# Three changes in one: two steps laid out in the program before the loop, transposes from a norm written in reverse, and fuller filler matmuls behind the first adder

## The chip, the cores and the metric

The kernel runs on one core of a Trainium2 chip. The metric is device time in microseconds (us) of one execution, as the median of three runs. Every value is float32 on a grid of 128 partitions: 4 images times 32 channels; a token is one of the 784 pixels.

## The reference

Four residual blocks follow each other on `x` of shape (4, 32, 28, 28):

```
x = x + conv_block(ln(x))       # 1x1 conv, adder 1 (-sum |x - w|), bn, relu, 3x3 conv, adder 2 (3x3), bn, relu
t = tokens(x); t = t + chain(ln(t))
x = x + quantised_convs(ln(x))  # two 3x3 convs with fake quantisation
t = tokens(x); t = t + stu(ln(t))   # 16 causal filters over time, then mixed by matrices; plus 3 lags

def step(h, p):                 # chain: a scan over 33 blocks
    op = argmax(h[0, 0, :19])
    y = attention(h, p, op);  h = where(p.am[op], y, h)
    z = ffn(h, p, op);        h = where(p.fm[op], z, h)
```

In the chain a block changes `h` only where its masks are set for the operation that the state itself picks. With these inputs two blocks change it: the first with its feed-forward part alone, the second with attention and feed-forward. The third decision says that nothing is left.

## The kernel before, in words

Each engine runs its own instruction stream, and semaphores order them. SP issues most DMAs, GpSimd sets up constants, and all matmuls are issued by the helper `mm` (L905), so that nearly every TensorE row of the profile carries that line. A float32 matmul stands in the trace as two weight loads and two matmuls.

**Adder 1 and what follows.** `group(g)` (L959) sums eight rings of `max(x, w)` or `|x - w|` into banks 6 and 7. A product of one column signals `adder_done`, and `SHORT` = 7 more of them follow (L980). ScalarE turns the banks into `H1P` (L369), and 9 taps of a convolution read `H1P` (L984 to L990, 144 matmul rows). Its result is copied by ScalarE (L374) and VectorE (L716), and 72 groups of adder 2 follow. `keep_warm(n)` issues n full filler products of 128x128 by 128x196, whose result nobody reads.

**The steps.** VectorE's `decide` (L763) writes a code into `KINT`: 0 for nothing left, bit 0 for attention, bit 1 for feed-forward. SP, ScalarE, VectorE and TensorE each load it into a register and walk `active_steps` (L74 to L89): three nested hardware loops of 3, 4 and 3 passes, with an `If(code > 0)` at each level, and the body of a step inside the innermost. The body stands once in each engine's program. After the last step the loops still run out: the innermost goes round once more, the middle one three times, the outer one twice, each pass branching over what is inside. In the body, `If((c & 1) > 0)` (L1030 on TensorE, L793 on VectorE, L412 on ScalarE) branches over the attention part when its bit is not set; `If((c & 2) > 0)` (L1133 on TensorE) does so for feed-forward. SP's `fetch` (L248) reads the code and issues the DMAs of the step's weights: `W4R` (L257), `W1R` (L261), `W2S` (L263). At the end of a step each engine waits for `decided`, loads the code again (L1155, L1156 on TensorE) and goes round. Behind the loops ScalarE loads the table for the square root (L465), and TensorE begins `norm(2)` with the product with `CEN` (L933), which needs `x2_ready` from VectorE's `residual` (L778).

**The last block.** `norm(3)` on VectorE (L532) writes its result in two halves into `UPZ`, in order of time. ScalarE writes it reversed into `URV` (L478), and TensorE transposes eight pieces of `URV` into banks 4 and 5 (L1185 to L1189), four for each parity. ScalarE and VectorE copy the two banks into `UT` (L482, L888). Then TensorE runs `filtered(u)` for 64 units and `mixed(grp)` for 16 groups into banks 6 and 7. SP builds `ULAG` from `UPZ` by 12 DMAs once `ln_out` has reached 8 (L279); they are read at group 12. After `mixed(15)` VectorE adds banks 6 and 7 to the residual (L899), and SP stores the result.

Of the kernel before, what the change touches and what calls it, by code (L numbers as in the profile page):

```python
# [4 lines left out]

# [1 line left out]

# [11 lines left out]
ACT = mybir.ActivationFunctionType  # L19
# [3 lines left out]
P = 128  # L23
NIMG, C, SIDE = 4, 32, 28
T = SIDE * SIDE
QU = T // 4
HT = T // 2
# [1 line left out]
PS_ = SIDE + 2  # L29
PADF = 904  # L30
NB, NOPS, HID = 33, 19, 128
STEPS = (3, 4, 3)

WARM = dict(inputs=6, means=4, squares=2, deviations=4, choice=8, weights=8, exponentials=2, sums=2, copies=11, evictions=3, relus=4, values=3)
SHORT = 7
OPW = 1024
QT, NQ = 112, 7
NK = 16
# [32 lines left out]
DVE_UPTO = [g - a for g, a in enumerate(ACT_UPTO)]  # L71


@contextmanager  # L74
def active_steps(e, code):


    assert STEPS[0] * STEPS[1] * STEPS[2] >= NB
    with e.Fori(0, STEPS[0]):
        with e.If(e.snap(code, min_val=0, max_val=4 * NB + 7) > 0):  # L80
            with e.Fori(0, STEPS[1]):
                with e.If(e.snap(code, min_val=0, max_val=4 * NB + 7) > 0):
                    with e.Fori(0, STEPS[2]):
                        c = e.snap(code, min_val=0, max_val=4 * NB + 7)
                        with e.If(c > 0):
                            yield c
                        e.nop()
                e.nop()
        e.nop()  # L89


def build(nc, x, par, con, ws1, wa1c, wa1r, ws2, wa2c, wa2r, amt, fmt, fwa, fwb, aw,
          cw1, cw2, phe, pho, mpp, mpm, mu, out):
    with ExitStack() as ctx:
# [6 lines left out]
        PS = ctx.enter_context(nc.psum_tensor("PS", [P, 8, 512], F32))  # L101
# [8 lines left out]
        X1 = sb("X1", [P, T]); HSUM = sb("H", [P, PS_ * SIDE]); H = HSUM[:, 0:T]  # L110
# [29 lines left out]
        UT = WS2[:, 0:8, :]  # L140
# [27 lines left out]
        def half(ap, h):  # L168
            return ap[:, h * HT:(h + 1) * HT]
# [9 lines left out]
        def bank(b, w=HT, rows_=slice(0, P)):  # L179
            return PS[rows_, b, 0:w]  # L180
# [17 lines left out]
        def by_image(src, n, c0=0, w=None):  # L198
# [12 lines left out]
            "wexp w_fill w_soft u_mixed w_chain sg_ready d_chain d_ready lags_in ut_done ut_ready urv_ready u_done uev_act uev_dve mix_done y_ready stored"  # L211
# [6 lines left out]
        def _(sp):  # L218
# [25 lines left out]
            code = sp.alloc_register("sp_code"); which = sp.alloc_register("sp_which")  # L244
# [21 lines left out]
            sp.wait_ge(s["decided"], 1)  # L266
            fetch()
            sp.reg_mov(chosen, 1)
            with active_steps(sp, code):
                n = sp.snap(chosen, min_val=1, max_val=NB)  # L270
                sp.wait_ge(s["decided"], n + 1)
                sp.sem_inc(s["sp_woke"], 1)
                sp.reg_add(chosen, chosen, 1)
                fetch()

            sp.wait_ge(s["ln_out"], 8)
            for b in range(NIMG):
                for lag in range(3):
                    sp.dma_start(ULAG[32 * lag:32 * lag + 32, b, :], UPZ[32 * b:32 * b + 32, 2 - lag:2 - lag + T]).then_inc(s["lags_in"], 16)  # L279
# [49 lines left out]
        def _(a):  # L329
# [49 lines left out]
            for n in range(9 * CQ):  # L379
# [10 lines left out]
                if n in (63, 66):  # L390
                    i = (n - 63) // 3
# [19 lines left out]
            with active_steps(a, code) as c:  # L411
                with a.If((c & 1) > 0):  # L412
                    k = a.snap(na, min_val=0, max_val=NB)

# [47 lines left out]
                a.load(code, KINT[0:1, 0:1], bass_reorder=False)  # L462
                a.reg_mov(code, a.snap(code) & (OPW - 1))

            a.activation(WSM[:, 44:45], con_("eps6", 1), ACT.Sqrt)  # L465
            norm(2, "eps6")

# [3 lines left out]
                    a.activation(half(SQ, h), bank(4 + h), ACT.Relu, bias=QS[:, 10 + i:11 + i],  # L471
                                 scale=QS[:, 8 + i:9 + i]).then_inc(s["cv_relu"], 1)
            norm(3, "eps5")
            a.wait_ge(s["zeroed"], 5)
            for h in range(2):
                a.wait_ge(s["ln_out"], 6 + h + 1)
                lo = h * HT
                a.activation(URV[:, 1024 - lo - HT:1024 - lo], UPZ[:, 2 + lo + HT - 1:2 + lo - 1:-1],  # L478
                             ACT.Copy).then_inc(s["urv_ready"], 1)

            a.wait_ge(s["ut_done"], 1)
            a.activation(UT[:, 0:4, :], PS[:, 4, 0:512].rearrange("p (i m) -> p i m", i=4), ACT.Copy).then_inc(s["ut_ready"], 1)  # L482
            for u in range(0, 64, 2):
                a.wait_ge(s["u_done"], u + 1)
                if u >= 8:
# [5 lines left out]
        def _(v):  # L491
# [23 lines left out]
            def norm(k, src, dst, between=None, after=None):  # L515

                for h in range(2):
                    if k == 0:
                        v.wait_ge(s["ln_mean"], h + 1)
                        v.tensor_tensor(half(XC, h), half(src, h), bank(h), ALU.subtract).then_inc(s["ln_cent"], 1)  # L520
                    else:
                        v.wait_ge(s["ln_sq"], 2 * k + h + 1)
                        v.tensor_copy(half(XC, h), bank(h)).then_inc(s["ln_cent"], 1)
                if between:
                    between()
                v.wait_ge(s["ln_sd"], k + 1)
# [263 lines left out]
            with active_steps(v, code) as c:  # L790
                past()
                look_ahead()
                with v.If((c & 1) > 0):  # L793
# [62 lines left out]
                v.load(code, KINT[0:1, 0:1], bass_reorder=False)  # L856
                v.reg_mov(code, v.snap(code) & (OPW - 1))

            norm(2, X, lambda h: half(XN, h))

            def hold(src, recip, low, high, tmp):
# [21 lines left out]
                v.tensor_tensor(X1[:, :], X[:, :], RS[:, :], ALU.add).then_inc(s["x3_sum"], 1)  # L883

            v.wait_ge(s["zeroed"], 5)
            norm(3, X1, lambda h: UPZ[:, 2 + h * HT:2 + (h + 1) * HT], None, summed)
            v.wait_ge(s["ut_done"], 2)
            v.tensor_copy(UT[:, 4:8, :], PS[:, 5, 0:512].rearrange("p (i m) -> p i m", i=4)).then_inc(s["ut_ready"], 1)  # L888
            for u in range(1, 64, 2):
                v.wait_ge(s["u_done"], u + 1)  # L890
                if u >= 8:
                    v.wait_ge(s["mix_done"], u // 4 - 1)
                v.tensor_copy(UEV[:, u % 8, :], bank(u % 6)).then_inc(s["uev_dve"], 1)  # L893
            v.wait_ge(s["mix_done"], 16)
            v.wait_ge(s["x3_sum"], 1)
            x3 = X1[:, :].rearrange("p (t a) -> p t a", a=2)
            y = Y1[:, :].rearrange("p (t a) -> p t a", a=2)
            for a2 in range(2):
                v.tensor_tensor(y[:, :, a2], x3[:, :, a2], bank(6 + a2), ALU.add).then_inc(s["y_ready"], 1)  # L899


        @block.tensor
        def _(t):
            def mm(out_, lhsT, rhs, start=True, stop=True):
                return t.matmul(out_, lhsT, rhs, start=start, stop=stop, skip_group_check=True)  # L905

            def keep_warm(n, src=CON, b=3):

                for _ in range(n):
                    mm(bank(b, QU), src[:, 0:P], src[:, 0:QU])  # L910
# [66 lines left out]
            for g in range(CQ):  # L977
                group(g)
            mm(PS[0:1, 5, 500:501], CON[:, 0:1], CON[:, 0:1]).then_inc(s["adder_done"], 1)
            for _ in range(SHORT):  # L980
                mm(PS[0:1, 5, 500:501], CON[:, 0:1], CON[:, 0:1])
            t.wait_ge(s["ws_rep"], 10)
            t.wait_ge(s["h1_ready"], 2)
            for tap in range(9):  # L984
# [43 lines left out]
            with active_steps(t, code) as c:  # L1028
                keep_warm(WARM["weights"])
                with t.If((c & 1) > 0):  # L1030
                    k, n = t.snap(na, min_val=0, max_val=NB), t.snap(chosen, min_val=1, max_val=NB)
# [10 lines left out]
                    for u in range(2 * NQ):  # L1042
                        j, h = u // 2, u % 2
# [111 lines left out]
                t.load(code, KINT[0:1, 0:1], bass_reorder=False)  # L1155
                t.reg_mov(code, t.snap(code) & (OPW - 1))  # L1156

            n = t.snap(chosen, min_val=1, max_val=NB + 1)
            t.wait_ge(s["x2_ready"], n)
            norm(2, X)  # L1160
# [183 lines left out]
```

## Time and profile before

| | us |
|---|---|
| median of 3 runs (384.72 to 385.14) | 384.8 |
| the profiled execution, its own time | 383.83 |
| its span, first to last instruction | 382.0 |
| TensorE matmuls busy | 346.2 (91%) |
| VectorE busy | 231.9 (61%) |
| ScalarE busy | 166.1 (43%) |

The span is taken apart by the profile; 1.8 us of the execution's own time lie outside it. The chain of waits is the path, followed back from the last instruction, of what released what. Busy time of TensorE holds fillers too, so it says little of what bounds the kernel. The granted clock is the share of full speed that TensorE was given: 1.0 is 2.4 GHz and 0.5 is 1.2 GHz.

### The profile page before, as it was taken

To read this page: it belongs to the slowest core of one execution; us is meant where nothing else is said; L and a number is where in the kernel's file an instruction comes from. 1 tells how busy PE (TensorE), PEld (TensorE's weight loads), DVE (VectorE), ACT (ScalarE), POOL (GpSimd) and SP (SyncE) were. 2 spreads that over 40 slices of the span, in tenths; PEclk is the share of its full clock that TensorE was granted. 3 is DMA by queue.
4 is the path that set the end of the run, shared out by engine and by line. 5 is a ranking of instruction groups with operands and counts; after the bars stand their busy time and mean duration, and the time that the engine had idled before them with its cause. 6 is when DMAs were issued, how large, how long until landed. Compare 5 with 4: busy or idle time off the path is not lost.

```text
span 382.0 us, 11465 instructions
## 1 busy us (share of the span) xinstructions
PE 346.2 (91%) x5075; PEld 201.3 (53%) x5075; DVE 231.9 (61%) x287; ACT 166.1 (43%) x161; POOL 20.2 (5%) x40
## 2 busy tenths in 40 slices
PE   8898999999999998695579998578799999999995
PEld 7535547743333346471153343454566667677773
DVE  2787999999999986559975785256411112121112
ACT  2851897888898931430018775213211111111110
POOL 4490000000000011000000000000000000000000
PEclk9998999999999999999999999899999999999998
DMA  5618000000000009000000000000320000000001
GB/s 164 213 22 307 33 2 2 2 2 3 2 2 2 2 8 330 16 16 2 0 2 2 0 2 2 0 2 0 72 58 3 3 3 3 3 3 3 3 3 44
DMA packets 10184, 12.79 MB, mean 33 GB/s; under 512 B 4102, under 2 KB 8984, under 8 KB 10136
## 3 DMA queue, kind: packets, MB, share of 16 engines
q1 hardware_dynamic: 9160, 8.85, 7.5%
q0 software_dynamic: 832, 3.00, 2.3%
q8 instruction: 42, 0.69, 0.7%
q10 hardware_dynamic: 144, 0.20, 0.2%
q14 instruction: 6, 0.05, 0.0%
HBM read 10.44 MB, written 0.40 MB: 28 GB/s over the span
## 4 chain that ended last, share of the span: by engine, by line
PE 76%; DVE 9%; issue 6%; DMA 2%; ACT 2%; SPq 1%; DVEq 0%; ACTq 0%
PE PS L905 76%; DVE TOPS L800 4%; DVE RSC L527 1%; DMA W1R<-in_fwa 1%; DMA W4R<-in_aw 1%; DVE pool_ L849 1%; DVE TMP L716 1%; DVE pool_ L744 0%; DVE pool_ L568 0%; ACT pool_ L438 0%; ACT SDC L338 0%; ACT H1P L369 0%; DVE X L759 0%; DVE TMP L757 0%; SPq L250 0%
## 5 line engine op out<-in xcount | busy, mean ns | idle before, releaser
L905 PE MATMUL PS<-pool_,CON 128*32 128x392 f32 (+2 forms) x1320 | 110.2, 493 | 0.6 <-DVE pool_ L744 0.4
L396 ACT ACTIVATE pool_<-TMP,WA 128x3136 f32<-128x3136 f32 x27 | 78.1, 2924 | 12.2 <-PE PS L905 11.4
L744 DVE TENSOR_SCALAR pool_<-TMP,WA 128x3136 f32<-128x3136 f32 x45 | 81.3, 1849 | 0.1
L905 PEld LDWEIGHTS PS<-pool_,CON 128*32 128x32 f32 (+1 forms) x1320 | 49.5, 110 | 59.2 <-issue 46.4
L893 DVE COPY pool_<-PS 128x392 f32<-128x392 f32 x32 | 18.1, 567 | 83.2 <-PE PS L905 83.2
L487 ACT ACTIVATE pool_<-PS 128x392 f32<-128x392 f32 x32 | 15.9, 498 | 85.0 <-PE PS L905 85.0
L905 PE MATMUL PS<-HE,WS 128*32 128x136 f32 (+3 forms) x1024 | 46.3, 333 | 0.8 <-DVE WS L888 0.8
L905 PE MATMUL PS<-pool_,WS 128*32 128x136 f32 (+3 forms) x1024 | 46.3, 333 | 0.0
L905 PEld LDWEIGHTS PS<-HE,WS 128*32 128x32 f32 x1024 | 31.9, 110 | 15.8 <-issue 10.8
L905 PEld LDWEIGHTS PS<-pool_,WS 128*32 128x32 f32 x1024 | 32.1, 110 | 14.8 <-issue 10.8
L905 PE MATMUL PS<-CON 128*128 128x196 f32 (+2 forms) x208 | 37.1, 323 | 2.1 <-DVE TOPS L800 0.8
L905 PEld LDWEIGHTS PS<-CON 128*128 128x128 f32 (+1 forms) x208 | 32.6, 184 | 10.2 <-issue 6.3
L438 ACT ACTIVATE pool_<-PS 112x896 f32<-112x896 f32 (+1 forms) x28 | 21.6, 822 | 6.3 <-PE PS L905 6.3
L800 DVE TENSOR_REDUCE TOPS<-PS 112x4 f32<-112x1568 f32 x14 | 23.9, 1783 | 0.3 <-PE PS L905 0.3
L905 PE MATMUL PS<-Y,QZ 32*112 32x392 f32 x112 | 12.9, 532 | 9.5 <-DVE TOPS L800 9.5
L821 DVE TENSOR_TENSOR pool_<-pool_ 112x1792 f32<-112x1792 f32 (+1 forms) x9 | 16.3, 1810 | 5.2 <-ACT pool_ L438 5.1
L905 PE MATMUL PS<-QZ,Y 32*112 32x448 f32 (+1 forms) x112 | 15.7, 531 | 0.3 <-ACT pool_ L438 0.3
L905 PE MATMUL PS<-pool_,ASEG 128*32 128x49 f32 (+2 forms) x512 | 14.4, 248 | 0.1
L905 PEld LDWEIGHTS PS<-Y,QZ 32*112 32x112 f32 x112 | 4.0, 169 | 18.4 <-DVE TOPS L800 17.2
L905 PE MATMUL PS<-pool_,VT 112*32 112x448 f32 (+1 forms) x112 | 12.0, 502 | 0.0
L420 ACT ACTIVATE VT<-PS 112x896 f32<-112x896 f32 x1 | 0.9, 918 | 25.1 <-PE PS L905 25.1
L905 PEld LDWEIGHTS PS<-QZ,Y 32*112 32x112 f32 x112 | 6.1, 169 | 9.2 <-issue 6.5
(215 smaller groups left out, 287.2 us busy)
## 6 DMA issues: line engine op xcount, KB each, us to landing
pool_<-in_pho SPq DMA_DIRECT2D x1, 3144.0 KB, 11.7
HE<-in_phe SPq DMA_DIRECT2D x1, 3136.0 KB, 10.4
QZ<-CW SPq DMA_DIRECT2D x12, 98.0 KB, 2.2
CW<-in_cw POOLq DMA_DIRECT2D x2, 576.0 KB, 4.7
CON<-in_con POOLq DMA_DIRECT2D x1, 732.5 KB, 5.6
out_y<-Y SPq DMA_DIRECT2D x1, 392.0 KB, 3.0
CQ<-in_ws SPq DMA_DIRECT2D x16, 9.0 KB
MPP<-in_mpp POOLq DMA_DIRECT2D x1, 256.0 KB, 2.9
```

The source lines that it names most:

```text
L396: a.activation(RING[:, g % RG, :, :].rearrange("p b (r c) -> p b r c", r=SIDE), window(n // CQ), ACT.Abs, bias=WA2[:, n:n + 1], scale=-1.0 ...
L420: a.activation(VT[0:QT, :, :], PS[0:QT, 4:8, 0:C * NQ], ACT.Copy).then_inc(s["v_done"], 1)
L438: a.activation(PT[0:QT, st % PR, 2 * pair:2 * pair + 2, 0:QC[ch]], PS[0:QT, 2 * (u % 3):2 * (u % 3) + 2, 0:QC[ch]], ACT.Exp, scale=SCALE). ...
L487: a.activation(UEV[:, u % 8, :], bank(u % 6), ACT.Copy).then_inc(s["uev_act"], 1)
L527: v.reciprocal(RSC[:, :], SDC[:, :]).then_inc(s["ln_rs"], 1)
L716: v.tensor_copy(inner(0, 1, 4)[64 * c:64 * c + 64], PS[64:128, 0:4, 0:HT].rearrange("p b (r c) -> p b r c", r=HROWS)).then_inc(s["y2_ready ...
L744: v.tensor_scalar(RING[:, g % RG, :, :].rearrange("p b (r c) -> p b r c", r=SIDE), window(n // CQ), WA2[:, n:n + 1], None, ALU.max).then_i ...
L800: v.tensor_reduce(TOPS[0:QT, u, :], PS[0:QT, 4 - 4 * (u % 2):8 - 4 * (u % 2), 0:HT], AX.X, ALU.max).then_inc(s["top_step"], 1)
L821: v.tensor_tensor(ACC[0:QT, :, 0:w], PT[0:QT, (st - 1) % PR, :, 0:w] if i == 1 else ACC[0:QT, :, 0:w], PT[0:QT, st % PR, :, 0:w], ALU.add) ...
L849: v.tensor_scalar(HIDT[:, u, :], bank(u), B1S, 0.0, ALU.add, ALU.max).then_inc(s["hid_dve"], 1)
L893: v.tensor_copy(UEV[:, u % 8, :], bank(u % 6)).then_inc(s["uev_dve"], 1)
L905: return t.matmul(out_, lhsT, rhs, start=start, stop=stop, skip_group_check=True)
```

## The change

Three edits are made together.

1. `active_steps` takes the body as a function and emits it three times: twice in a row, each behind an `If(code > 0)`, and a third time inside two nested loops (4 and 8 passes), all of it inside the second `If`'s successor. A code of 0 after the second step branches over the loops and the third copy.
2. `norm(3)` writes its result reversed, straight into `URV`. TensorE transposes the first piece of each parity after the first half (`ln_out` 7), the other six after the second. It starts the filters when ScalarE's half of `UT` is there, and waits for VectorE's half at unit 4. ScalarE writes `UPZ` from `URV` afterwards, in one instruction, and SP's 12 DMAs wait for that. At the end, the addition of bank 6 waits for `mixed(13)` only.
3. Behind adder 1, four full filler products replace seven of one column.

```diff
-STEPS = (3, 4, 3)
+STEPS = (4, 8)
-def active_steps(e, code):
-    with e.Fori(0, STEPS[0]):
-        with e.If(e.snap(code, min_val=0, max_val=4 * NB + 7) > 0):
-            with e.Fori(0, STEPS[1]):
-                with e.If(e.snap(code, min_val=0, max_val=4 * NB + 7) > 0):
-                    with e.Fori(0, STEPS[2]):
-                        c = e.snap(code, min_val=0, max_val=4 * NB + 7)
-                        with e.If(c > 0):
-                            yield c
-                        e.nop()
-                e.nop()
-        e.nop()
+def active_steps(e, code, step):
+    def taken():
+        return e.snap(code, min_val=0, max_val=4 * NB + 7)
+    with e.If(taken() > 0):
+        step(taken())
+        with e.If(taken() > 0):
+            step(taken())
+            with e.If(taken() > 0):
+                with e.Fori(0, STEPS[0]):
+                    with e.If(taken() > 0):
+                        with e.Fori(0, STEPS[1]):
+                            c = taken()
+                            with e.If(c > 0):
+                                step(c)
+                            e.nop()
+                    e.nop()
...
 # SP, before the 12 DMAs
-            sp.wait_ge(s["ln_out"], 8)
+            sp.wait_ge(s["u_plain"], 1)
...
 # ScalarE
             norm(3, "eps5")
-            a.wait_ge(s["zeroed"], 5)
-            for h in range(2):
-                a.wait_ge(s["ln_out"], 6 + h + 1)
-                lo = h * HT
-                a.activation(URV[:, 1024 - lo - HT:1024 - lo], UPZ[:, 2 + lo + HT - 1:2 + lo - 1:-1],
-                             ACT.Copy).then_inc(s["urv_ready"], 1)
             a.wait_ge(s["ut_done"], 1)
-            a.activation(UT[:, 0:4, :], ...).then_inc(s["ut_ready"], 1)
+            a.activation(UT[:, 0:4, :], ...).then_inc(s["ut_act"], 1)
+            a.wait_ge(s["zeroed"], 5)
+            a.wait_ge(s["ln_out"], 8)
+            a.activation(UPZ[:, 2:2 + T], URV[:, 1023:1023 - T:-1], ACT.Copy).then_inc(s["u_plain"], 1)
...
 # VectorE
-            norm(3, X1, lambda h: UPZ[:, 2 + h * HT:2 + (h + 1) * HT], None, summed)
+            norm(3, X1, lambda h: URV[:, 1023 - h * HT:1023 - (h + 1) * HT:-1], None, summed)
...
-            v.wait_ge(s["mix_done"], 16)
             for a2 in range(2):
+                v.wait_ge(s["mix_done"], 14 + 2 * a2)
                 v.tensor_tensor(y[:, :, a2], x3[:, :, a2], bank(6 + a2), ALU.add).then_inc(s["y_ready"], 1)
...
 # TensorE
-            for _ in range(SHORT):
-                mm(PS[0:1, 5, 500:501], CON[:, 0:1], CON[:, 0:1])
+            keep_warm(WARM["shifts"], b=5)      # WARM["shifts"] = 4
...
-            t.wait_ge(s["ln_out"], 8)
-            t.wait_ge(s["urv_ready"], 2)
+            t.wait_ge(s["ln_out"], 7)
             for c in range(2):
-                for i in range(4):
-                    a0 = 1024 - 255 - c - 256 * i
-                    last = mm(PS[:, 4 + c, P * i:P * i + P], URV[:, a0:a0 + 255:2], con_("ident"))
+                turned(c, 0)
+            t.wait_ge(s["ln_out"], 8)
+            for c in range(2):
+                for i in range(1, 4):
+                    last = turned(c, i)
                 last.then_inc(s["ut_done"], 1)
-            t.wait_ge(s["ut_ready"], 2)
             t.wait_ge(s["strip_in"], 32)
+            t.wait_ge(s["ut_act"], 1)
...
+                if u == 4:
+                    t.wait_ge(s["ut_dve"], 1)
```

`turned(c, i)` is the transpose that stood in the loop before.

## Rows read from the trace of the kernel before

**Rows 1.** The chain that ended last; columns: start us, us, what.
```profile
44.44 97.42 PE PS L905 x1159
...
157.13 1.52 issue
...
165.61 3.04 DMA W4R<-in_aw
...
241.66 4.12 issue
...
275.14 101.37 PE PS L905 x2230
```
**Rows 2.** Timeline of TensorE's matmuls behind adder 1: start us, us.
```profile
28.69 0.54 PE L905 MATMUL PS<-CON 128*1 128x1 f32 x16
30.83 7.88 PE L905 MATMUL PS<-H1P,WS 32*64 32x392 f32 x144 [1.60 <-ACT H1P L369]
```
**Rows 3.** Busy time by stretch; after POOL stand PEclk, DMA share, GB/s.
```profile
31.20:34.50 3.30, 3.30 (x49) 1.95 (x41) 3.02 (x13) 0.00 (x0) 0.00 (x0) 0.50 1.04 383
34.60:38.60 4.00, 4.00 (x104) 2.27 (x88) 1.85 (x7) 0.00 (x0) 0.00 (x0) 1.00 1.06 391
```
**Rows 4.** Timeline of TensorE, four full filler products at full clock.
```profile
146.89 1.59 PE L905 MATMUL PS<-CON 128*128 128x196 f32 x8
```
**Rows 5.** Timeline of VectorE, the first copy after the convolution.
```profile
38.88 1.79 DVE L716 COPY TMP<-PS 64x1568 f32<-64x1568 f32 x1 [2.29 <-PE PS L905]
```
**Rows 6.** TensorE's sequencer in front of step 1, by line: min/median/max ns, start us.
```profile
L80 PEldq COMPARE_BRANCH  x1: 94/94/94, 153.3 to 153.3; - x1
...
L85 PEldq COMPARE_BRANCH  x1: 65/65/65, 153.9 to 153.9; - x1
...
L1030 PEldq COMPARE_BRANCH  x1: 3832/3832/3832, 154.2 to 154.2; - x1
```
**Rows 7.** Busy time and instructions in step 2: its attention, then all of it.
```profile
168.60:234.50 65.90, 54.73 (x567) 22.71 (x567) 50.20 (x40) 27.15 (x38) 0.00 (x0) 1.00 0.01 2
165.40:241.00 75.60, 63.24 (x632) 28.99 (x632) 56.71 (x53) 31.38 (x45) 0.00 (x0) 1.00 0.01 3
```
**Rows 8.** The loops' end on TensorE's sequencer (first and last line) and DMA, 236 to 256.
```profile
L83 PEldq COMPARE_BRANCH  x2: 76/150/223, 240.7 to 241.4; - x2
...
L79 PEldq COMPARE_BRANCH  x3: 76/207/208, 244.1 to 245.6; - x3
...
DMA packets 0, 0.00 MB, mean 0 GB/s; under 512 B 0, under 2 KB 0, under 8 KB 0
```
**Rows 9.** Timeline of ScalarE behind the loops.
```profile
244.22 1.28 ACT L465 ACT_TABLE_LOAD   x1 [4.78 <-issue]
```
**Rows 10.** Two products with CEN in norm 2, and the same two in norm 3.
```profile
245.79 2.60 PE L905 MATMUL PS<-X,CEN 128*128 128x392 f32 x4 [4.12 <-issue]
...
258.69 1.48 PE L905 MATMUL PS<-X,CEN 128*128 128x392 f32 x4
```
**Rows 11.** Busy time and clock behind the loops, columns as in rows 3.
```profile
246.20:249.60 3.40, 3.40 (x8) 1.98 (x6) 1.14 (x2) 1.00 (x2) 0.00 (x0) 0.50 0.00 0
```
**Rows 12.** Timelines of TensorE, VectorE and ScalarE between norm 3 and the filters.
```profile
272.23 2.12 PE L905 MATMUL PS<-CON,CW 128*128 128x128 f32 x16 [1.31 <-ACT CW L478]
...
270.30 1.23 DVE L532 TENSOR_TENSOR CW<-TMP,PS 128x392 f32<-128x392 f32 x2 [0.20 <-PE PS L905]
274.39 0.69 DVE L888 COPY WS<-PS 128x512 f32<-128x512 f32 x1 [2.87 <-PE PS L905]
...
270.95 1.14 ACT L478 ACTIVATE CW<-CW 128x392 f32<-128x392 f32 x2 [3.09 <-DVE CW L532]
273.45 0.60 ACT L482 ACTIVATE WS<-PS 128x512 f32<-128x512 f32 x1 [1.36 <-PE PS L905]
```
**Rows 13.** Timeline of VectorE at the end.
```profile
375.89 0.57 DVE L893 COPY pool_<-PS 128x392 f32<-128x392 f32 x1 [2.23 <-PE PS L905]
377.55 1.04 DVE L899 TENSOR_TENSOR Y<-X,PS 128x392 f32<-128x392 f32 x2 [1.09 <-PE PS L905]
```

More of the change, by code:

```diff
@@ L8 @@
-from contextlib import ExitStack, contextmanager
+from contextlib import ExitStack
 import concourse.bass as bass
@@ L31 @@
 NB, NOPS, HID = 33, 19, 128
-STEPS = (3, 4, 3)
-WARM = dict(inputs=6, means=4, squares=2, deviations=4, choice=8, weights=8, exponentials=2, sums=2, copies=11, evictions=3, relus=4, values=3)
-SHORT = 7
+STEPS = (4, 8)
+WARM = dict(inputs=6, means=4, squares=2, deviations=4, choice=8, weights=8, exponentials=2, sums=2, copies=11, evictions=3, shifts=4, relus=4, values=3)
 OPW = 1024
@@ L71 @@
 DVE_UPTO = [g - a for g, a in enumerate(ACT_UPTO)]
-@contextmanager
-def active_steps(e, code):
-    assert STEPS[0] * STEPS[1] * STEPS[2] >= NB
-    with e.Fori(0, STEPS[0]):
-        with e.If(e.snap(code, min_val=0, max_val=4 * NB + 7) > 0):
-            with e.Fori(0, STEPS[1]):
-                with e.If(e.snap(code, min_val=0, max_val=4 * NB + 7) > 0):
-                    with e.Fori(0, STEPS[2]):
-                        c = e.snap(code, min_val=0, max_val=4 * NB + 7)
-                        with e.If(c > 0):
-                            yield c
-                        e.nop()
-                e.nop()
-        e.nop()
+def active_steps(e, code, step):
+    def taken():
+        return e.snap(code, min_val=0, max_val=4 * NB + 7)
+    assert 2 + STEPS[0] * STEPS[1] >= NB
+    with e.If(taken() > 0):
[11 more added lines that the diff above has]
+                    e.nop()
 def build(nc, x, par, con, ws1, wa1c, wa1r, ws2, wa2c, wa2r, amt, fmt, fwa, fwb, aw,
@@ L210, in build @@
             "wmx_part wmx_rows wmx_row wmx_bc q_sc q_chain cq_chain cq_done x2_ready q_xin cc_done cv_relu cv_q x3_ready x3_sum "
-            "wexp w_fill w_soft u_mixed w_chain sg_ready d_chain d_ready lags_in ut_done ut_ready urv_ready u_done uev_act uev_dve mix_done y_ready stored"
+            "wexp w_fill w_soft u_mixed w_chain sg_ready d_chain d_ready lags_in ut_done ut_act ut_dve u_plain u_done uev_act uev_dve mix_done y_ready stored"
         ).split()}
@@ L268, in _, with step @@
             sp.reg_mov(chosen, 1)
-            with active_steps(sp, code):
+            def step(c):
                 n = sp.snap(chosen, min_val=1, max_val=NB)
@@ L274, in _ @@
                 fetch()
-            sp.wait_ge(s["ln_out"], 8)
+            active_steps(sp, code, step)
+            sp.wait_ge(s["u_plain"], 1)
             for b in range(NIMG):
@@ L410, in _, with step @@
             a.reg_mov(chosen, 1)
-            with active_steps(a, code) as c:
+            def step(c):
                 with a.If((c & 1) > 0):
@@ L463, in _ @@
                 a.reg_mov(code, a.snap(code) & (OPW - 1))
+            active_steps(a, code, step)
             a.activation(WSM[:, 44:45], con_("eps6", 1), ACT.Sqrt)
@@ L473, in _ @@
             norm(3, "eps5")
+            a.wait_ge(s["ut_done"], 1)
+            a.activation(UT[:, 0:4, :], PS[:, 4, 0:512].rearrange("p (i m) -> p i m", i=4), ACT.Copy).then_inc(s["ut_act"], 1)
             a.wait_ge(s["zeroed"], 5)
-            for h in range(2):
-                a.wait_ge(s["ln_out"], 6 + h + 1)
-                lo = h * HT
-                a.activation(URV[:, 1024 - lo - HT:1024 - lo], UPZ[:, 2 + lo + HT - 1:2 + lo - 1:-1],
-                             ACT.Copy).then_inc(s["urv_ready"], 1)
-            a.wait_ge(s["ut_done"], 1)
-            a.activation(UT[:, 0:4, :], PS[:, 4, 0:512].rearrange("p (i m) -> p i m", i=4), ACT.Copy).then_inc(s["ut_ready"], 1)
+            a.wait_ge(s["ln_out"], 8)
+            a.activation(UPZ[:, 2:2 + T], URV[:, 1023:1023 - T:-1], ACT.Copy).then_inc(s["u_plain"], 1)
             for u in range(0, 64, 2):
@@ L789, in _, with step @@
             v.reg_mov(na, 0); v.reg_mov(nf, 0)
-            with active_steps(v, code) as c:
+            def step(c):
                 past()
@@ L857, in _ @@
                 v.reg_mov(code, v.snap(code) & (OPW - 1))
+            active_steps(v, code, step)
             norm(2, X, lambda h: half(XN, h))
@@ L885, in _ @@
             v.wait_ge(s["zeroed"], 5)
-            norm(3, X1, lambda h: UPZ[:, 2 + h * HT:2 + (h + 1) * HT], None, summed)
+            norm(3, X1, lambda h: URV[:, 1023 - h * HT:1023 - (h + 1) * HT:-1], None, summed)
             v.wait_ge(s["ut_done"], 2)
-            v.tensor_copy(UT[:, 4:8, :], PS[:, 5, 0:512].rearrange("p (i m) -> p i m", i=4)).then_inc(s["ut_ready"], 1)
+            v.tensor_copy(UT[:, 4:8, :], PS[:, 5, 0:512].rearrange("p (i m) -> p i m", i=4)).then_inc(s["ut_dve"], 1)
             for u in range(1, 64, 2):
@@ L1027, in _, with step @@
             t.reg_mov(chosen, 1)
-            with active_steps(t, code) as c:
+            def step(c):
                 keep_warm(WARM["weights"])
@@ L1156, in _ @@
                 t.reg_mov(code, t.snap(code) & (OPW - 1))
+            active_steps(t, code, step)
             n = t.snap(chosen, min_val=1, max_val=NB + 1)
@@ L1182, in direct, with turned @@
                 return last
-            t.wait_ge(s["urv_ready"], 2)
+            def turned(c, i):
+                a0 = 1024 - 255 - c - 256 * i
+                return mm(PS[:, 4 + c, P * i:P * i + P], URV[:, a0:a0 + 255:2], con_("ident"))
+            t.wait_ge(s["ln_out"], 7)
             for c in range(2):
-                for i in range(4):
-                    a0 = 1024 - 255 - c - 256 * i
-                    last = mm(PS[:, 4 + c, P * i:P * i + P], URV[:, a0:a0 + 255:2], con_("ident"))
+                turned(c, 0)
[3 more added lines that the diff above has]
+                    last = turned(c, i)
                 last.then_inc(s["ut_done"], 1)
-            t.wait_ge(s["ut_ready"], 2)
             t.wait_ge(s["strip_in"], 32)
+            t.wait_ge(s["ut_act"], 1)
             def filtered(u):
```

## The prediction, made before the changed kernel ran

> **What bounds the kernel now.** I read the page for the busy shares, then the chain of waits, then the timelines, sequencer rows and granted clock at each of the three places that the change touches. On the chain the reader should see two kinds of piece. Adder 2 is one TensorE piece of 97.42 us and the filters one of 101.37 us [rows 1]: nothing in the change touches their inside, so a microsecond gained ahead of either arrives whole at the end. Between them lie short serial stretches, and two of the longest waits there are called "issue": 1.52 us before the first feed-forward and 4.12 us behind the last step [rows 1]. The sequencer's rows say what these are. In front of step 1, TensorE's branch over the attention part took 3.832 us [rows 6], against 65 and 94 ns for branches not taken. Behind step 2 the loops run out in a dozen branches of 76 to 223 ns, from 240.7 to 245.7, and no DMA packet moves meanwhile [rows 8]: their targets were on the engine already. So a branch costs either about 0.2 us or nearly 4, and the question of this change is which kind the new exit is.
>
> **Fillers behind adder 1.** Removed are seven products of one column, which with the signal take 0.54 us and end at 29.23; TensorE then waits 1.60 us for `H1P` and starts at 30.83 [rows 2]. From 31.2 to 34.5 it is granted half its clock, later all of it [rows 3]. Four full fillers take 1.59 us [rows 4]; from about 28.76 (one eighth of the 0.54 is the signal's) they end at 30.35, still 0.48 before the convolution can start, so they cost nothing. Past that cover each further filler would cost 0.4. They leave a gap of 0.5 us instead of 1.6, and I expect the clock to hold. At half clock 41 weight loads passed in 3.30 us, at full clock 88 in 4.00 or a little less, since they stop before the stretch ends [rows 3]: 0.045 us each, so the 41 would take 1.86 at most and 1.65 at exactly double speed. The gain is 1.44 to 1.65. Bounds: nothing, if the clock falls anyway, and 1.65. The copies behind find their engine free: VectorE idled 2.29 us before its one [rows 5]. I take **1.6**, since a convolution that only TensorE carries should follow its clock.
>
> **Entering step 1.** The loop set-up between the branches at L80 (153.3) and L85 (153.9) goes [rows 6]: 0.6 us. The branch over attention stays, over the same distance, and its 3.83 us begin 0.6 earlier. TensorE is ready at 158.05 instead of 158.65. The weights landed at 157.13 [rows 1], so they don't take the place of the stall until 1.5 us are gone. Gain **0.6**; bounds 0 (the fetch ends no earlier) and 1.5 (the landing). Between the steps nothing is gained: step 2 starts when `W4R` lands, 3.04 us after its issue at 165.61 [rows 1], SP issues it inside the body, and TensorE's fillers cover the loop's turn.
>
> **Leaving step 2.** The dozen branches become one move and one branch at about 240.65. Its target lies behind a third copy of the body. Step 2 executed 632 matmuls and as many weight loads, its attention part alone 567 of each [rows 7]. The branch that skipped those 567 pairs was not resident and took 3.83 us; this one skips 632 pairs, code that never ran. I therefore price it at the same 3.83: it ends at 244.48, and norm 2 starts 0.15 later, at 244.63, instead of 245.79 [rows 10]. Gain **1.16**. Bounds: with a resident target 0.2 us, so that TensorE starts at 241.75, after its last filler (the wait of 4.12 begins at 241.66 [rows 1]), gain 4.0; with a second fetch behind the first, up to another 3.83, loss 2.7. ScalarE loads its table at 244.22 [rows 9] and is ready at 245.7. In the new kernel a short jump there lets it load from 240.9; were its jump as long as TensorE's, it would still load at 244.2, and its first square needs TensorE's product, not before 245.4. VectorE and SP have more time than that. So TensorE sets it.
>
> The Trainium skill, page "Runtime: NRT & Kernel Launch", section "Instruction fetch mechanics", says that prefetch is sequential in blocks, and that a taken branch outside the current two pages stalls for a fetch. For the new exit that gives the same result as my 3.83. It also would make most backward and forward branches of the old exit stalls; this trace measured 76 to 223 ns for them, so here the measurement decides, and the old exit is priced at what it took.
>
> **The clock behind the exit.** The wait of 4.12 us was followed by half clock from 246.2 to 249.6 [rows 11]: the two products with `CEN` took 2.60 us, where norm 3's took 1.48 [rows 10]. The new wait is 3.0 us (241.66 to 244.63). A wait of 1.6 behind adder 1, after thin products, was enough for a fall. I take it to stay: **0**. If it doesn't, between 1.1 (the products alone) and 1.7 (half of 3.4) is gained; 1.4 is the middle.
>
> **Before the filters.** Now: VectorE's halves end at 270.87 and 271.53, ScalarE reverses the second until 272.10, eight transposes take 2.12 us from 272.23, VectorE's copy ends at 275.08 [rows 12], filters at 275.14 [rows 1]. New: the transposes of the first piece run from 271.0 to 271.5, beside VectorE's second half. From 271.63 the remaining six take 12 of 16 rows' time, 1.5. ScalarE's bank is complete after three (0.72 to the last start, 0.3 for it): its copy runs 272.65 to 273.25 (0.60 [rows 12]), and the filters start at 273.30. VectorE's copy of the other bank ends before 274.1 and is needed four units of 64 later, 6.3 of the 101.37 us. Gain **1.84**. The price of writing backwards on VectorE isn't in the trace; nearest is its last addition, which writes every second element at 0.52 us each for 392 [rows 13], and ScalarE's reversed read at 0.57. I take nothing; doubled writes would cost 1.2 at most. ScalarE's new whole write of `UPZ`, about 1.1 us by its two old ones [rows 12], ends at 274.4, before the first unit wants evicting, one 64th of 101.37 us behind 273.30, at 274.9. The 12 DMAs move about 2.8 us later; their data are read at group 12, some 75 us on, so they cost nothing, and it would take that much delay before they cost.
>
> **The end.** Bank 6's addition moves ahead of `mixed(15)`: VectorE is free at 376.46, the pair now starts at 377.55 and takes 1.04 [rows 13]. One of the two is hidden. Gain **0.5**; bounds 0 and 0.52.
>
> **The sum.** 1.6 + 0.6 + 1.16 + 0 + 1.84 + 0.5 = 5.7 us. The profiled execution of 383.83 (1.8 outside its span) becomes 378.1. The median of the runs lies 1.0 above that execution, so the median goes from 384.8 to 379.1.
>
> **Rivals.**
> - *The exit's target is resident.* For it: every branch of the old exit was. Against it: the skip over a shorter stretch in step 1 wasn't. TensorE starts 2.85 us sooner than forecast and idles too little for the clock to fall: 379.1 - 2.85 - 1.4 = 374.8. The skill's "Advanced Engine Details and Errata", section "ISA Cache", gives TensorE 128 KB; were code resident that far ahead, this would be the case.
> - *The clock holds behind the exit.* The wait is a quarter shorter. 379.1 - 1.4 = 377.7.
> - *The fillers don't hold the clock behind adder 1*, so the edit does not do what it could: 379.1 + 1.6 = 380.7. For it: a gap of 0.5 us stays; against it: that is a third of the old one, and the work ahead of it is no longer thin.
> - *A second fetch behind the exit.* The landing is near the end of a block, and the next one arrives late: up to 3.83 us more on the path, 381 to 383. Even whole it doesn't undo the sum.
> - *Slower: step 2's attention stalls on its own instructions.* It is now a second copy, reached in a straight line behind a first that was skipped. If it meets two stalls like that of [rows 6], 7.7 us are lost and the kernel ends at 384.8 - 5.7 + 7.7 = 386.8; one leaves it faster, the second decides. Against it: in the old kernel too its attention ran for the first time in step 2, and TensorE was busy there for 54.73 of 65.90 us [rows 7], which leaves little room for stalls.
>
> **Chances.** Forecast as it stands 0.48; clock holds behind the exit 0.17; fillers without effect 0.11; second fetch 0.10; resident target 0.07; slower or no gain by step 2's fetches 0.07. The range goes from 377.0 to 381.6: it holds the first three cases and the nearer part of the second fetch, about 0.8. Under 0.2% (0.77 us) this kernel's measurement cannot tell from no change. Faster 0.93, same 0.03, slower 0.04.
>
> **What would show it.** Clock 1.0 from 31 to 35, and the convolution at about 6.3 us instead of 7.88. A branch of about 3.8 us on TensorE at the new kernel's exit, an instruction packet within it, and norm 2 starting about 3 us after the last filler. Transposes in two pieces, and under 2.5 us from VectorE's first half to the filters, instead of 4.3. One addition behind the last matmul. Wrong it would be through a short exit branch, a second long branch or idle "issue" in norm 2, or "issue" inside step 2.

## The result and the profile after

The changed kernel took 379.56 us on the median of 4 executions (378.59 to 381.2), against 384.97 for the kernel before: a ratio of 0.9856 with a 95% interval of 0.9811 to 0.9900. The forecast was 379.1, in a range of 377.0 to 381.6, faster. With six further executions the changed kernel's median over ten is 379.03, and that of the kernel before over the 62 that ran beside the experiments is 384.70. The ratios, here and below, compare fast executions alone, those within 1.5% of the fastest of the same kernel. The single executions scatter far more than the three shown at first: those 62 lie between 380.33 and 387.82.

One number that comes with each execution orders most of this scatter: its mean granted clock. Of the 62, the twelve with 0.99 or more have a median of 381.24, the thirty with 0.98 or less one of 385.97. The profiled execution of the changed kernel took 381.2 at 0.964, the slowest of its four; the forecast for it had been 378.1. Its stages have to be compared one by one.

First the chain of the changed kernel, from the start of the convolution; columns as in [rows 1].

```profile
30.25 6.26 PE PS L915 x144
...
42.17 97.41 PE PS L915 x1159
...
154.87 1.03 issue
...
162.13 0.46 issue
...
163.38 3.15 DMA W4R<-in_aw
...
193.76 8.75 PE PS L915 x89
...
243.69 2.42 issue
...
273.62 101.39 PE PS L915 x2201
```

The two long pieces are as long as before [rows 1]. The convolution is 1.7 us shorter than in [rows 2]. Both "issue" pieces at the far branches are there, shorter, and one of 0.46 is new: SP pauses between reading the code and issuing the weights of step 2. Next TensorE's sequencer at the two far branches; columns as in [rows 6].

```profile
L1040 PEldq COMPARE_BRANCH  x1: 3917/3917/3917, 151.4 to 151.4; - x1
...
L84 PEldq COMPARE_BRANCH  x1: 3342/3342/3342, 242.6 to 242.6; - x1
```

The branches of the loops' end, of which [rows 8] show the first and last lines (15 by all of them, not the dozen of the prediction), have become one of 3.34 us. The DMA view from 242.6 to 246.0 holds this row: one instruction packet of 0.02 MB, and narrower windows place it between 243.5 and 243.7, inside the branch.

```profile
q8 instruction: 1, 0.02, 1.9%
```

ScalarE's, VectorE's and SP's own branches of the same line took 0.05, 0.056 and 0.045 us. The stall is TensorE's alone.

Then the clock, by stretch; columns as in [rows 3].

```profile
31.20:34.50 3.30, 3.30 (x88) 2.10 (x80) 3.02 (x15) 0.00 (x0) 0.00 (x0) 1.00 1.03 376
175.00:192.00 17.00, 15.27 (x80) 4.29 (x76) 16.57 (x11) 0.00 (x0) 0.00 (x0) 0.50 0.01 1
195.40:202.00 6.60, 6.60 (x40) 5.26 (x40) 1.81 (x8) 1.46 (x2) 0.00 (x0) 0.50 0.00 0
246.60:249.90 3.30, 3.30 (x8) 1.89 (x7) 1.13 (x2) 0.99 (x2) 0.00 (x0) 0.50 0.03 7
```

Behind adder 1 the clock holds now, 80 weight loads in a stretch that had 41 [rows 3]. In norm 2 it falls as before [rows 11]. New against the profile before is half clock for 17 us in the row maxima of attention and for nearly 7 behind them. Last, the end of norm 3 and of the kernel, in the timelines of TensorE, ScalarE and VectorE; these answer to [rows 12] and [rows 13].

```profile
271.21 2.35 PE L915 MATMUL PS<-CON,CW 128*128 128x128 f32 x16
273.62 5.75 PE L915 MATMUL PS<-HE,WS 128*32 128x392 f32 x125
...
272.88 0.60 ACT L486 ACTIVATE WS<-PS 128x512 f32<-128x512 f32 x1 [4.72 <-PE PS L915]
...
270.59 1.23 DVE L539 TENSOR_TENSOR CW<-TMP,PS 128x392 f32<-128x392 f32 x2 [0.19 <-PE PS L915]
273.59 0.69 DVE L898 COPY WS<-PS 128x512 f32<-128x512 f32 x1 [1.77 <-PE PS L915]
...
374.88 0.56 DVE L909 TENSOR_TENSOR Y<-X,PS 128x392 f32<-128x392 f32 x1
376.06 0.56 DVE L909 TENSOR_TENSOR Y<-X,PS 128x392 f32<-128x392 f32 x1 [0.61 <-PE PS L915]
```

Writing backwards costs VectorE nothing: 1.23 us for two halves, as in [rows 12]. The filters start 3.03 us after VectorE begins its first half; before it was 4.84.

Stage by stage, worked out from the starts and ends in both kernels' timelines (us):

| stage | before | after | difference | forecast |
|---|---|---|---|---|
| start to convolution | 30.83 | 30.25 | -0.58 | 0 |
| convolution | 7.88 | 6.19 | -1.69 | -1.6 |
| first decision to feed-forward | 6.84 | 6.39 | -0.45 | -0.6 |
| second decision to projections | 5.26 | 5.87 | +0.61 | 0 |
| projections to third decision | 70.67 | 74.82 | +4.15 | 0 |
| third decision to norm 2 | 6.11 | 4.41 | -1.70 | -1.16 |
| norm 2, to its last product | 7.93 | 7.90 | -0.03 | 0 |
| then to the filters | 21.42 | 19.61 | -1.81 | -1.84 |
| filters to the last addition's end | 103.45 | 102.99 | -0.46 | -0.5 |

With -0.01 over the stages not shown, this adds up to the 1.97 us by which the last addition ends sooner (378.59 to 376.62). The 0.58 at the start is no edit's gain: two profiles of the changed kernel have 30.25 and 30.47, and those of the kernels below lie between 30.21 and 31.25, with either kind of product behind adder 1. Nor is the rest of the profiled execution's gain (2.63 us in all): the store of the result landed 2.4 us after its issue instead of 3.0, and it took 2.4 or 2.5 in every kernel below, whatever its edits.

### The profile page after: what moved, and what is told of

The parts are those of the page before. It is cut to its first block, busy times and chain, and to the rows that moved or that the text cites. A ratio compares the mean times of both kernels' runs of the same rounds, so it can differ in the third digit from the quotient of the medians.

```text
span 379.4 us, 11303 instructions
## 1 busy us (share of the span) xinstructions
PE 354.3 (93%) x5069; PEld 211.7 (56%) x5069; DVE 231.5 (61%) x287; ACT 165.8 (44%) x160; POOL 19.6 (5%) x40
## 4 chain that ended last, share of the span: by engine, by line
PE 79%; DVE 8%; issue 4%; DMA 2%; ACT 1%; SPq 1%; DVEq 0%; ACTq 0%
PE PS L915 79%; DVE TOPS L808 3%; DVE RSC L534 1%; DMA W1R<-in_fwa 1%; DMA W4R<-in_aw 1%; DVE pool_ L857 1%; DVE TMP L723 1%; DVE pool_ L751 0%; DVE pool_ L575 0%; ACT pool_ L446 0%; ACT SDC L345 0%; ACT H1P L376 0%; DVE X L766 0%; DVE TMP L764 0%; SPq L254 0%
## 5 line engine op out<-in xcount | busy, mean ns | idle before, releaser
L915 PE MATMUL PS<-HE,WS 128*32 128x392 f32 (+3 forms) x1024 | 46.5, 333 | 0.1
L915 PE MATMUL PS<-CON 128*128 128x196 f32 (+1 forms) x202 | 40.2, 346 | 2.4 <-DVE TOPS L808 0.9
L915 PEld LDWEIGHTS PS<-pool_,WS 128*32 128x32 f32 x1024 | 35.8, 110 | 11.2 <-issue 3.5
L915 PEld LDWEIGHTS PS<-HE,WS 128*32 128x32 f32 x1024 | 35.6, 111 | 11.6 <-issue 4.1
L915 PEld LDWEIGHTS PS<-CON 128*128 128x128 f32 x202 | 35.2, 200 | 10.3 <-issue 5.4
L915 PE MATMUL PS<-Y,QZ 32*112 32x392 f32 x112 | 19.6, 786 | 3.6 <-DVE TOPS L808 3.4
L915 PE MATMUL PS<-QZ,Y 32*112 32x448 f32 (+1 forms) x112 | 16.6, 563 | 0.3 <-ACT pool_ L446 0.3
L915 PEld LDWEIGHTS PS<-Y,QZ 32*112 32x112 f32 x112 | 5.6, 241 | 17.5 <-DVE TOPS L808 16.4
```

## The experiments

The theory was: each edit acts by itself, the exit waits for a fetch of code that lies too far ahead, and the large remainder is TensorE's clock. The rivals: the exit waits for other things; the new layout itself brings the clock down in attention; the fillers' gain was chance.

**Each edit alone, on the kernel before.** The edits are the three parts of the diff in the section on the change.

> The kernel before with the filler edit alone. My account: the convolution behind adder 1 runs at full clock, in 6.2 us instead of 7.9, and the kernel gains 1.4 to 1.7 us (about 383.3). Rival: the low clock there was chance and the kernel before often runs without it; then the gain over many runs is under 0.5 us.

Measured: 383.99 us (12 executions, 382.42 to 387.6), ratio 1.0019 (0.9977 to 1.0061). Its profile has the convolution in 6.19 us; the timing can't tell a gain.

> The kernel before with the program's layout of the steps alone. My account, from the changed kernel's rows: about 0.45 us gained in front of step 1, about 0.6 lost between the steps, 1.2 to 1.7 gained at the exit, where TensorE's branch takes 3.3 to 3.9 us; together 1 to 1.7 us, about 383.5. Rival: the straight layout also causes the half clock in the row-max stage that the changed kernel's profile shows from 175 to 202 us; then this kernel is no faster on the median, and its mean clock is low in several runs.

Measured: 382.41 us (12 executions), ratio 0.9926 (0.9879 to 0.9972). In its profile 0.53 us are gained in front of step 1 and 0.49 lost between the steps; the exit branch is 3.62 us long, and the way from the decision to norm 2 takes 4.69 instead of 6.11. The row maxima ran at full clock, from 170 to 193 us:

```profile
170.00:193.00 23.00, 13.54 (x124) 4.12 (x116) 21.57 (x15) 0.81 (x3) 0.00 (x0) 1.00 0.00 1
```

So the layout doesn't bring the clock down there by itself. Behind the row maxima this profile has half clock too, from 195.5 to 201.5. The kernel with the filler edit alone, whose layout is the old one, shows the same fall there; the mean over 9 us is 0.62:

```profile
193.00:202.00 9.00, 9.00 (x92) 7.21 (x91) 3.13 (x8) 2.06 (x3) 0.00 (x0) 0.62 0.01 2
```

> The kernel before with the edits of the last block alone. My account: filters start 1.8 us sooner and the last addition ends 0.45 sooner, 2.3 us together, about 382.5, in every run alike since nothing of it hangs on the clock. Rival: the backward write or the later 12 DMAs cost something that the single profile hides; then under 1.8.

Measured: 381.88 us (12 executions), ratio 0.9966 (0.9923 to 1.0009), unclear as a time. In its profile both stages are as forecast: 19.62 us from norm 2 to the filters, 103.00 from there to the last addition. It also ran the convolution behind seven thin products, the case in which the clock was to fall, at full clock:

```profile
28.23 0.54 PE L902 MATMUL PS<-CON 128*1 128x1 f32 x16
30.36 6.19 PE L902 MATMUL PS<-H1P,WS 32*64 32x392 f32 x144 [1.58 <-ACT H1P L369]
```

By their medians the three kernels are 0.7, 2.3 and 2.8 us below the kernel before beside them (384.68). That adds up to 5.8, near the whole, but by the ratios only 3.4 us are found, and the scatter is too large to prove a sum. The terms are told apart by the stages of the profiles, not by these times.

**The distance at the exit.** The changed kernel, but the third copy of the step leaves out attention:

```diff
                             with e.If(c > 0):
+                                LITE[0] = True
                                 step(c)
+                                LITE[0] = False
...
-                with t.If((c & 1) > 0):
+                if not LITE[0]:          # likewise on ScalarE and VectorE
+                    with t.If((c & 1) > 0):
```

> The changed kernel with the attention part left out of the third copy of the step, which these inputs never reach, so that the exit branch on TensorE passes over some 75 pairs of instructions instead of 640. If the exit waits for the fetch of a far target: its branch takes under 0.3 us or at most a part of a fetch, norm 2 starts 2 to 3 us sooner after the third decision, and 2 to 4 us are gained against the changed kernel (376 to 377.5), the upper end if the clock then holds behind the exit. Rival: the exit waits for something else (the residual, the table load, the sequencer's bookkeeping): no change, 379.5.

Measured: 376.06 us (6 executions, 372.39 to 377.23), ratio 0.9797 (0.9738 to 0.9857). Its exit branch took 0.35 us and norm 2 follows the last filler with no idle time and at full clock, as its TensorE timeline shows:

```profile
236.25 2.92 PE L922 MATMUL PS<-CON 128*128 128x196 f32 x16
239.01 1.48 PE L922 MATMUL PS<-X,CEN 128*128 128x392 f32 x4
```

From the start of the last product that reads `W2S` to the decision it took 1.73 us in both kernels, and ScalarE still loads its table. Only the distance changed, so the exit's stall comes from the distance. Against the changed kernel's profile the stage up to norm 2 gave 2.58 us and norm 2 itself 1.74.

**Announcing the branch.** All copies whole; one instruction ahead of step 2 tells TensorE's sequencer which branch is coming.

```diff
+@contextmanager
+def far_if(nc, e, cond, mark, name):
+    e.br_cond(cond, name + "_in", name + "_out").branch_hint(mark)
+    with nc.body(name + "_in", valid_engines=[e.engine]):
+        yield
+        e.br(name + "_out")
+    nc.switch_bb(name + "_out")
...
         with e.If(taken() > 0):
+            exit_mark = e.mark_branch_hint_location() if nc else None
             step(taken())
-            with e.If(taken() > 0):
+            with far_if(nc, e, taken() > 0, exit_mark, "more_steps") if nc else e.If(taken() > 0):
```

> The changed kernel, all three copies of the step kept, with one added instruction on TensorE: ahead of step 2 it announces the branch that leaves for norm 2, so that the target's code can be fetched before the branch is reached. If the stall is a fetch that comes too late: the branch takes under 0.5 us instead of 3.3, and the kernel is near the one with the short third copy, 376 to 377. Rival: the announcement comes too far ahead, or its fetch takes the place of the next block that step 2 needs: no gain, or a stall inside step 2 that shows as issue on the chain.

Measured: 374.54 us (6 executions), ratio 0.9747 (0.9713 to 0.9780). The branch took 0.381 us instead of 3.342, with every copy in place, and norm 2 began 1.83 us after the decision. Then the branch over attention in step 1 as well:

```diff
+            skip_mark = t.mark_branch_hint_location()
             norm(1, X1, "x1_ready")
...
-                with t.If((c & 1) > 0):
+                with far_if(nc, t, (c & 1) > 0, mark, "attention") if mark else t.If((c & 1) > 0):
```

> As the kernel with the announced exit, and the branch over attention in step 1 is announced too, ahead of norm 1. If that stall is the same fetch: TensorE's branch falls from 3.9 us to under 0.5, the first feed-forward starts when its weights land, about 1 us sooner than in the changed kernel, and no more than that. Rival: the block behind a skipped attention has to be fetched again when step 2 runs; then what step 1 gains is lost in front of step 2's attention.

Measured: 371.90 us (6 executions, 371.29 to 375.15), ratio 0.9690 (0.9654 to 0.9725). The sequencer's branches of step 1 and of the exit, and TensorE's first feed-forward:

```profile
L76 PEldq COMPARE_BRANCH  x1: 467/467/467, 151.3 to 151.3; - x1
...
L76 PEldq COMPARE_BRANCH  x1: 372/372/372, 241.0 to 241.0; - x1
...
155.05 1.60 PE L926 MATMUL PS<-H,W1R 32*128 32x392 f32 x16 [1.05 <-DMA W1R<-in_fwa]
```

Step 1 now waits for its weights, which is the bound that the prediction gave; from decision to feed-forward it is 5.57 instead of 6.39.

> The kernel with both branches announced, again: 371.5 to 373.5 on the median if the first result was no chance; 7 us below the changed kernel, of which 2.9 to 4.3 at the exit, 1 in step 1, 1.1 to 1.7 of clock in norm 2, and the rest fewer falls of the clock elsewhere.

Measured: 375.09 us (6 executions), ratio 0.9739 (0.9693 to 0.9785); both stages as before (5.50 and 1.83). The two medians of one kernel differ by 3.2 us, more than the 1.7 that the fillers behind adder 1 could gain. Over the twelve executions the median is 374.3, and neither series alone is the number.

**Filling time for the clock.** Fillers moved from the start of a step to the end of the one before; and one filler in each turn of the row maxima.

```diff
-choice=8, weights=8
+choice=14, weights=2
```

> The changed kernel with six of the eight fillers at the start of a step moved to the end of the step before, in front of the decision: behind the last step 14 fillers run instead of 8, 5.1 us instead of 2.9, and cover most of the exit's stall. If the half clock in norm 2 comes from the idle stretch: it is gone, norm 2 takes 6.4 us instead of 7.9, 1.1 to 1.7 us gained. Rival: TensorE's queue is too short for 14 products, its sequencer reaches the code later, and the stall begins later: then the gain is eaten or turned into a loss.

Measured: 379.01 us (6 executions), ratio 0.9850 (0.9804 to 0.9896): no gain in time. In its profile the clock in norm 2 held and norm 2 took 6.26 us instead of 7.90; but it took 6.26 too in two profiles of the same exit with 8 fillers, so this doesn't show that the fillers held it. 1.74 us of the stall stayed uncovered (the timeline, then the exit branch):

```profile
239.59 4.91 PE L915 MATMUL PS<-CON 128*128 128x196 f32 x28
246.23 1.58 PE L915 MATMUL PS<-X,CEN 128*128 128x392 f32 x4 [1.74 <-issue]
...
L84 PEldq COMPARE_BRANCH  x1: 3867/3867/3867, 242.2 to 242.2; - x1
```

Its branch took 3.87 us, and the sequencer reached it 1.7 us after the third decision (240.52 to 242.2), where it had been 0.9 in the changed kernel (241.70 to 242.6). That is the rival named above: behind 14 fillers the stall begins 0.8 us later. With the longer branch it makes the way from the decision to norm 2 5.71 us instead of 4.41, so what the fillers cover isn't gained.

```diff
                             t.wait_ge(s["top_step"], k * 14 + (u - 1))
+                            keep_warm(1, b=4 - 4 * h)
```

> The changed kernel with one full filler in each of the 12 later turns of the row-max stage of attention, behind the wait for VectorE. There TensorE works 0.93 of each 1.70 us, and its clock fell to half in some executions, which made VectorE wait 3.3 to 4 us in all. If too little work is what lets the clock fall: the mean clock of nearly all runs is above 0.985, the slow third of the runs is gone, and the median gains 1 to 2 us. Rival: the filler, 0.39 us in front of each turn, delays VectorE by itself: up to 12 times 0.1 us lost and the scatter as before.

Measured: 378.79 us (6 executions), ratio 0.9848 (0.9818 to 0.9879). The clock was 0.991 or 0.995 in all six, where the ten executions of the changed kernel went from 0.964 to 1.000; the median gain that was expected isn't shown. In its profile the row maxima ran at full clock, but half clock came behind them and again in norm 2. Its exit branch took 4.67 us, the longest of all.

> The changed kernel once more, for the number of its executions: its first four ran from 378.6 to 381.2 while the kernel before ran from 380.7 to 387.8 in 40. If the spread of both is that of the granted clock, its median is 378.5 to 380, and every execution below 378 has a mean clock of 0.99 or more.

Measured: 377.46 us (6 executions, 374.52 to 380.13), ratio 0.9797 (0.9735 to 0.9858); branches 3.76 and 3.94 us. The three executions under 377 have a mean clock of 1.000, the others 0.986 to 0.991. The median itself was a microsecond under what was expected.

> Both branches announced, 14 fillers in front of each decision, and one filler in each turn of the row-max stage. With both stalls gone there is nothing left for the 14 fillers to cover at the exit: they end later than the third decision by 5 us instead of 3 and delay norm 2 by 1 to 2 us. If the row-max filler holds the clock there, it returns 1 to 2 us on the executions in which it fell. Expected 372 to 374, no better than both announcements alone; under 371.5 would say that the clock is worth more than I take it for.

Measured: 374.98 us (6 executions), ratio 0.9745 (0.9696 to 0.9794), beside 375.09 for the two announcements alone on the same chip. From decision to norm 2 it took 3.82 us, 2 more than without the 14 fillers, and attention 70.59 us, at full clock, 1.6 less than in the second profile of the two announcements alone (72.20). By the profiles the one about pays for the other. Its sequencer reached the exit 1.7 us after the decision as well, and the announced branch was short:

```profile
L76 PEldq COMPARE_BRANCH  x1: 454/454/454, 238.2 to 238.2; - x1
```

> Both branches announced and one filler in each turn of the row-max stage, without the 14 fillers, which cost 2 us at the exit. From the stages measured so far: 1.83 us from the third decision to norm 2 instead of 3.82, and the clock held from the row maxima to the third decision (70.6 us instead of 72 to 74). Expected median 371 to 373.5, the lowest of all; 375 or more would say that the row-max filler holds nothing.

Measured: 375.87 us (6 executions, 372.51 to 379.58), ratio 0.9766 (0.9694 to 0.9838). That is a miss. The clock held in attention (70.57 us), but the announced exit branch took 2.791 us after all, and norm 2 fell to half clock behind it.

```profile
L76 PEldq COMPARE_BRANCH  x2: 382/1586/2791, 152.4 to 238.4; - x2
...
241.37 2.65 PE L926 MATMUL PS<-X,CEN 128*128 128x392 f32 x4 [2.03 <-issue]
```

The DMA views show where the packets moved, though not which code they brought. With both announcements alone one instruction packet of 0.02 MB moved between 230.7 and 233 us and none from 236 to 241.3, so none while the branch ran from 241.0. The changed kernel without an announcement had one between 232 and 236, and a second one inside its branch. Here no such packet moved between 228 and 238, and one did between 238.8 and 239.1, after the branch was reached at 238.4.

The twelve products put 48 instructions into each of the two copies ahead of the exit and so moved the branch. The kernel with the announcements, the row-max fillers and the 14 fillers has the same twelve, and six more ahead of the exit, another 24 instructions. There the packet moved between 235.5 and 237, ahead of the branch at 238.2, and the branch was short. The rows suggest that an announcement is acted on only when the engine comes to the branch's own part of the code, and that with the row-max fillers alone this was at the branch. That isn't shown: no run moved the branch and nothing else.

## Why the prediction was right, point by point

- *Fillers, 1.6 us.* The mechanism is right in the profile: half clock goes, 1.69 us, just above the bound of 1.65. The gap left before the convolution was 0.99 us instead of 0.5 (0.41 to 1.02 in the eleven profiles with full fillers). Full clock held there in all eleven, and in one of three without. So the term is a gain in some executions only, and alone it wasn't measurable (1.0019, 0.9977 to 1.0061). The step took a clock seen in one execution for the rule.
- *Entering step 1, 0.6.* Measured 0.45; the branch was 0.09 longer.
- *Between the steps, nothing.* This failed: 0.61 lost, 0.50 of it on SP's way from the decision to issuing `W4R`, where the chain shows the pause of 0.46. From decision to issue it took 2.36 to 2.39 us in every kernel with copies and 1.86 or 1.87 in the three with the loops alone. The remaining 0.11 is the landing, 3.15 us instead of 3.04. The prediction said that SP issues inside the body and therefore at the same distance; it didn't price the instructions' place in SP's own program. Why SP pauses exactly there stays open.
- *Leaving step 2, 1.16.* The decisive step held. The branch was long (3.34), since its target was far, and 1.70 were gained; the half microsecond above the forecast is the shorter branch, which took 3.3 to 4.7 us in the five profiles with such an exit instead of one fixed 3.83. In a second profile of the changed kernel it took 3.94, and the gain was 1.09. The Trainium skill, "Runtime: NRT & Kernel Launch", section "Instruction fetch mechanics", says that a taken branch whose target isn't in the current window of two pages waits for a DMA fetch. The rows of the two far branches agree; those of the old exit don't, as the prediction noted. The same section says that kernels prefer full unrolling where possible; here the copy that never runs is what lay under the jump.
- *Clock behind the exit, 0.* Right for this profile (7.90 us), and not a rule. The length of the wait, from which it was argued, doesn't order the profiles: the clock fell behind waits of 2.03, 2.42, 3.90 and 4.12 to 4.17 us and held behind 1.74, 2.70 and 3.02 (6.26 us each). It held in all where norm 2 followed without a pause. The 1.4 us stated for it measured 1.54 to 1.74 against this profile; norm 2 took 7.54 and 8.64 us in two others with a fall.
- *Before the filters 1.84 and the end 0.5.* Measured 1.81 and 0.46; the same within 0.04 in every profile with these edits. They don't depend on the clock of a short stretch, and were the safest terms of the sum.
- *Not in the sum: attention's clock.* The profile lost 4.15 us there. It's no cost of the layout: attention took 70.67, 72.47 and 73.81 us in the three profiles with the loops alone. With copies, and full clock as in the 70.67, it took 70.57 to 70.75 in three profiles (two of them with the row-max fillers), so the second copy brought no fetch stalls into step 2 either, which was the rival "slower".
- *Rivals.* The resident target was wrong as a forecast, but priced what became possible: 374.8 forecast, 374.54 and 376.06 measured. A second fetch behind the exit didn't show. That the fillers behind adder 1 have no effect isn't borne out by the profiles; for the median it stays open.
- *Resolution.* 0.2% was read from three executions that happened to lie within 0.42 us. In 62, the same kernel spans 7.5 us.
- *Luck.* The medians, 379.56 and over ten 379.03, lie within half a microsecond of the 379.1 that was forecast. The interval of the ratio is 1.7 us wide to either side, one term failed by 0.61 and another shows in some executions only. The profiled execution missed its forecast by 3.1 us, for a clock that the sum doesn't contain. So the closeness of the median is luck; that the terms of 1.69, 0.45, 1.70, 1.81 and 0.46 us stand in the stages is not.

## What to carry to other kernels

Look at sequencer rows wherever the chain says "issue": here a branch of 3 to 5 us was code being fetched, and whether it was paid depended on how much code lay under the jump, though that code never ran. Announce such a branch well ahead, or keep rare code out from under the common path, and check the branch's row again after every edit that shifts instructions. Compare the stages of profiles, and executions with a like clock, before believing a median of three.

## What was not expected of the hardware

The granted clock differed between executions of one program in the same stretch: two profiles of the changed kernel show the row maxima, and norm 2, at either level. So do the transition behind the row maxima and the convolution behind thin products in profiles of kernels that are alike, or nearly, up to there. Half clock over the transition (89 matmul rows) made it 8.75 us instead of 5.50. A far branch that was announced took 0.36 to 0.47 us in eight cases and 2.79 in one; one that wasn't took 3.34 to 4.67 (fifteen).

The fastest kernel measured is the changed one with both branches announced: medians of 371.90 and 375.09 us in two series, against 384.25 and 385.87 for the kernel before beside them.
